# GpSimd's row moves without waits for TensorE, a loading queue with stores between the first row loads, and gathers without a bound

## The chip, the cores and the metric

The kernel runs on one core of a Trainium2 chip. The time is the device time of one execution in microseconds: 1025.71 us is the median of three runs (1023.77, 1025.71 and 1027.04). A core has five engines with instruction queues of their own, TensorE (PE; its weight loads are PEld), VectorE (DVE), ScalarE (ACT), GpSimd (POOL) and SyncE (SP), and 16 DMA engines that all of them share. Queues run in order; they meet only at semaphores.

## The reference

Two transformer layers on 1024 tokens of width 256 (two sequences of 512), each with layer norm, attention and a mixture of experts, all in float32:

```python
x = x + _L0_attn_ref(_layernorm(x), ...)   # 16 heads, a triangular solve over the keys
x = x + _L0_ffn_ref(_layernorm(x), ...)    # 64 experts, top 8, capacity 256 rows each
x = x + _L1_attn_ref(_layernorm(x), ...)   # cumulative sum of phi(k) * v, 16 heads
x = x + _L1_ffn_ref(_layernorm(x), ...)    # 8 experts, top 2
```

The change lies around the first mixture of experts. What it computes:

```python
scores, idx = jax.lax.top_k(probs, TOP_K)                    # 8 experts for each token
xbuf = zeros((E, C, D)).at[e_sorted, pos].set(x[tok_sorted]) # rows sorted by expert
g = einsum('ecd,efd->ecf', xbuf, w_gate); u = einsum('ecd,efd->ecf', xbuf, w_up)
y = einsum('ecf,edf->ecd', silu(g) * u, w_down)
out = zeros((N, D)).at[tok_sorted].add(y_pair)               # each token adds its 8 rows
```

## The kernel before

The program has three blocks, and all five engines meet at a barrier at the end of each: an engine drains its queue, then waits for the others.

**First block: attention of layer 0.** It ends with VectorE choosing the eight experts of the first sequence's tokens (tiles 0 to 3 of 128 tokens) and their slots, while TensorE still works on attention. When those slots are there, GpSimd starts to scatter rows (`scatter`, line 198): one indirect DMA moves the 128 rows of tile `t` for their k-th expert into `expert_rows` in HBM. Experts are sorted within a token, so a row of expert e can only stand among k = 0 to e. There are 8 x 8 = 64 scatters, k by k: 32 for the first sequence, then 32 for the second. The first `EARLY` of them stand in the first block, the others in the second. Between some of them GpSimd waits for a state of TensorE (lines 1193 to 1204, 1527 to 1546); no data depends on these waits.

**Second block: the 64 experts of layer 0.** VectorE computes the slots of the second sequence. TensorE turns the rows of an expert (L1368), multiplies them with the gate and up weights (L1375), turns the hidden rows (L1383) and multiplies with the down weights (L1392); ScalarE applies SiLU, VectorE the product and the copy of the result to `yb` (L1468). The experts run one behind another, software pipelined: `turn` of e + 1, `gate_up` of e, `turn_hidden` of e - 1, `down` of e - 2. SyncE's queue does all loads and stores: weights of two experts at a time into four buffers (L1566, L1567), an expert's 256 rows into one of eight buffers (L1572), and the store of an expert's output (L1576). The load of rows e < 8 waits until all eight scatters of k = e have landed. The order in this queue is written by hand: three weight groups, rows 0 to 5, then a body of eight experts repeated eight times (`steps`; the middle ones as a loop).

At the end GpSimd gathers the outputs back: with row numbers `gather_slots` it fetches 128 rows for one tile and one k into one of 16 buffers `gb` (L1558). The first 16 gathers stand in this block. They wait for the stores that they read (semaphores `s_st`), and, one by one, for a state of TensorE (`s_gu`, `s_y0`). Each has a bound on its row numbers, beyond which it reports an error.

**Third block: layer 1.** VectorE adds the gathered rows into X (L1939), 16 first and then 12 in each of four quarters of two tiles; behind each quarter come its layer norm and linear attention: TensorE turns and projects (L1730, L1742), ScalarE computes features (L1874 to L1880), VectorE a window of cumulative sums (L1950 to L1957), two windows to a quarter, with three gathered adds ahead of the second. GpSimd issues the other 48 gathers (L2116), each as soon as its buffer is free and, at five places of a quarter, only after a state of TensorE. Then layer 1's own scatter (L2132), 23 tiles of expert work (L1815, L1824), each added to `out` by an indirect DMA that accumulates (L2141).

## Time and profile before

| | |
|---|---|
| median of three runs | 1025.71 us (1023.77 to 1027.04) |
| the profiled execution's own time | 1016.34 us |
| its span, first to last instruction | 1014.6 us |
| mean granted TensorE clock | 0.837 |
| busy: PE, PEld, DVE, ACT, POOL | 708.1, 566.9, 549.2, 313.5, 252.2 us |
| DMA | 151.73 MB, mean 150 GB/s |

All durations below are of the one profiled execution. A row of a timeline has the start in us, the duration in us, engine, line, operation, what it writes and reads, a count, and in brackets the idle time of the engine before it with what ended it. "issue" there means that nothing in the profile was waited for. An engine name with a q (SPq, POOLq) is the engine's instruction queue. A DMA's row on POOL is the time in which its descriptors are made, not the transfer.

### The profile page before, as it was taken

What the parts mean: (1) busy time and instruction counts of PE and PEld (TensorE: products, weight loads), DVE (VectorE), ACT (ScalarE), POOL (GpSimd) and SP (SyncE); (2) the same over time, 40 slices, a digit from 0 to 9 for tenths busy, and PEclk for the clock granted to TensorE, in tenths of its full rate; (3) what the DMA queues carried; (4) which work ended last, traced back from release to release, by engine and by line L of the source; (5) the groups of instructions that cost most, each with busy time, mean ns of one, the idle gap of its engine ahead of it and who ended that gap; (6) DMA issues with size and microseconds to landing.
All of it is one profiled execution on the core that took longest, in us unless ns stands there. A gap on an engine that the chain in (4) does not pass through costs nothing. (4 is left out here: it accounts for less than half of the span.)

```text
span 1014.6 us, 17699 instructions
## 1 busy us (share of the span) xinstructions
PE 708.1 (70%) x6542; PEld 566.9 (56%) x6587; DVE 549.2 (54%) x1652; ACT 313.5 (31%) x535; POOL 252.2 (25%) x258
## 2 busy tenths in 40 slices
PE   4858377858757786973156999999205763599995
PEld 2423265446436545842145999999204542599994
DVE  6896986799499679263501333333146675022221
ACT  1004143542444355432022444444003451111110
POOL 6003011120211111016762000000575626023222
PEclk9988779979887898597577999999756675699998
DMA  4981002340631358204947888887422204688760
GB/s 136 137 130 48 0 2 46 156 63 3 199 51 14 125 211 319 96 17 146 320 142 251 288 290 291 294 283 248 130 76 68 81 26 156 244 229 249 221 195 1
DMA packets 75561, 151.73 MB, mean 150 GB/s; under 512 B 12768, under 2 KB 36064, under 8 KB 72544
## 3 DMA queue, kind: packets, MB, share of 16 engines
q1 hardware_dynamic: 62064, 124.27, 39.7%
q0 software_dynamic: 10224, 21.12, 7.4%
q10 hardware_dynamic: 3200, 5.38, 1.6%
q8 instruction: 44, 0.72, 0.3%
q14 instruction: 29, 0.24, 0.1%
HBM read 91.01 MB, written 60.43 MB: 149 GB/s over the span
## 5 line engine op out<-in xcount | busy, mean ns | idle before, releaser
L1375 PE MATMUL scores<-wgu,zero 128*128 128x192 f32 x512 | 98.2, 337 | 3.7 <-DMA wd<-in_wd 3.7
L750 DVE TENSOR_REDUCE block_maxima<-scores 128x10 f32<-128x1280 f32 x64 | 92.3, 1486 | 7.7 <-PE scores L400 6.7
L1032 ACT ACTIVATE E<-scores 128x1280 f32<-128x1280 f32 x64 | 77.3, 1238 | 60.6 <-PE scores L411 32.4
L1476 DVE TENSOR_TENSOR gated_up<-gated,scores 128x192 f32<-128x192 f32 x64 | 22.7, 354 | 123.7 <-ACT gated L1517 123.7
L1375 PEld LDWEIGHTS scores<-wgu,zero 128*128 128x128 f32 x512 | 85.6, 197 | 3.9 <-DMA wd<-in_wd 3.9
L1815 PE MATMUL scores<-xgT,w 128*128 128x128 f32 x736 | 87.8, 278 | 0.0
L1815 PEld LDWEIGHTS scores<-xgT,w 128*128 128x128 f32 x736 | 86.0, 196 | 0.1
L1170 POOL TENSOR_SCALAR_AFFINE_SELECT E<-E 128x256 f32<-128x256 f32 x64 | 27.2, 449 | 205.8 <-ACT E L1032 205.7
L1508 ACT COPY zero<-misc 128x512 f32<-128x512 f32 x64 | 37.5, 586 | 98.3 <-PE misc L1368 98.3
L1392 PE MATMUL scores<-wd,gated_turned 96*128 96x256 f32 x256 | 67.0, 385 | 0.5 <-ACT gated_turned L1504 0.5
L2116 POOL DMA_INDIRECT gb<-expert_outputs,gather_slots x48 | 55.0, 1147 | 33.7 <-DVE X L1939 17.0
L1368 PE MATMUL misc<-cf,xg 128*128 128x128 f32 x256 | 40.3, 281 | 32.7 <-DMA xg<-expert_rows 32.7
L2141 POOL DMA_INDIRECT out<-yb,add_to x23 | 35.5, 1544 | 111.0 <-DVE yb L2079 109.0
L1558 POOL DMA_INDIRECT gb<-expert_outputs,gather_slots x16 | 16.4, 1024 | 171.5 <-DMA expert_outputs<-xnT 164.9
L1468 DVE COPY xnT<-scores 128x512 f32<-128x512 f32 x64 | 44.3, 692 | 25.6 <-PE scores L1392 25.6
L2092 DVE TENSOR_TENSOR cum<-low,scores 128x512 f32<-128x512 f32 x23 | 15.8, 689 | 77.2 <-issue 67.8
L1368 PEld LDWEIGHTS misc<-cf,xg 128*128 128x128 f32 x256 | 32.4, 144 | 41.5 <-issue 19.5
L400 PE MATMUL scores<-cb 128*128 128x128 bf16 x256 | 53.5, 230 | 1.8 <-issue 0.7
L825 DVE TENSOR_TENSOR tmp<-Y,LB 128x120 f32<-128x120 f32 (+35 forms) x244 | 49.7, 242 | 0.3
L834 DVE TENSOR_TENSOR Y<-Y,tmp 128x120 f32<-128x120 f32 (+35 forms) x244 | 49.6, 242 | 0.1
L199 POOL DMA_INDIRECT expert_rows<-stack_q,scatter_slots x32 | 31.5, 984 | 66.4 <-issue 61.3
L1392 PEld LDWEIGHTS scores<-wd,gated_turned 96*128 96x128 f32 x256 | 44.5, 194 | 4.4 <-ACT gated_turned L1504 0.7
(295 smaller groups left out, 1500.4 us busy)
## 6 DMA issues: line engine op xcount, KB each, us to landing
w<-in_w SPq DMA_DIRECT2D x23, 1024.0 KB, 5.0
expert_rows<-zero SPq DMA_DIRECT2D x32, 512.0 KB, 6.2
xg<-expert_rows SPq DMA_DIRECT2D x64, 256.0 KB, 3.2
expert_outputs<-xnT SPq DMA_DIRECT2D x64, 256.0 KB, 3.0
wgu<-in_wgu SPq DMA_DIRECT2D x32, 384.0 KB, 3.6
rows_by_expert<-zero SPq DMA_DIRECT2D x21, 408.0 KB, 6.0
wd<-in_wd SPq DMA_DIRECT2D x32, 192.0 KB, 3.8
w<-in_w ACTq DMA_DIRECT2D x8, 512.0 KB, 10.3
```

The costliest lines, as they stand in the source:

```text
L400: ins = nc.tensor.matmul(scores[:, slot, o + w - P:o + w], identb, mask[c, it], start=False, stop=True)
L750: nc.vector.tensor_reduce(bm[:, c, h, :], scores[:, slot, 0:WIDE].rearrange("p (a n) -> p a n", n=P), AX.X, ALU.max).then_inc(s_fd, 1)
L825: nc.vector.tensor_tensor(part, Yc[:, x, 0:n, k:k + 1].to_broadcast([P, n, w]), LB[:, k:k + 1, k + 1:SB].to_broadcast([P, n, w]), ALU.mult ...
L834: nc.vector.tensor_tensor(below, below, part, ALU.add).then_inc(s_inv, 1)
L1032: nc.scalar.activation(to[:, h, :], scores[:, k % 2, 0:WIDE], ACT.Exp, scale=SCALE).then_inc(s_fa, 1)
L1368: ins = nc.tensor.transpose(misc[:, j % 2, c:c + P], xg[:, j, t, k * P:(k + 1) * P], identf)
L1375: ins = nc.tensor.matmul(scores[:, j % 2, t * 2 * F0:(t + 1) * 2 * F0], xgT[:, j % 2, k, t * P:(t + 1) * P], wgu[:, j // GE, j % GE, k, :] ...
L1392: ins = nc.tensor.matmul(scores[:, j % 2, 1024 + t * D:1024 + (t + 1) * D], hT[:, j % 2, t * P:(t + 1) * P], wd[:, j // GE, j % GE, :], st ...
L1468: nc.vector.tensor_copy(yb[:, j % NY].rearrange("p t d -> p (t d)"), scores[:, j % 2, 1024:1536]).then_inc(s_yv, 1)
L1508: nc.scalar.copy(xgT[:, j % 2].rearrange("p k n -> p (k n)"), misc[:, j % 2, :]).then_inc(s_xt0, 1)
L1815: ins = nc.tensor.matmul(scores[:, j, c:c + P], w13[:, q, k, c:c + P], xgT[:, j, k, :], start=(k == 0), stop=(k == KT - 1))
L2116: pool.indirect_dma_start(out=gb[:, g % NG, :], out_offset=None, in_=ybuf, in_offset=bass.IndirectOffsetOnAxis(ap=ig[:, t, k:k + 1], axis= ...
```

## The change

`EARLY` goes from 16 to 10, so six scatters move behind the first barrier. GpSimd's waits for TensorE's states go in all three blocks; its waits for slots, stores and free buffers stay. Both gathers lose the bound on their row numbers (`bounds_check`, `oob_is_err`). TensorE waits for the slots (`s_idx`) where it waited for the picked weights (`s_w8`) before the first expert. SyncE loads four weight groups before the first rows, puts the stores of experts 0 to 2 between rows 4 to 7, and the first body of eight experts is written out in another order. The whole diff:

```diff
--- before.py
+++ after.py
@@ -40,7 +40,7 @@
 BIG = 32768.0
 LIN_AT = (0, 512, 256)
 LG = 1280
-EARLY = 16
+EARLY = 10
 NQ = 4
 GQ = (N // P // NQ) * 6
 W = N // NQ
@@ -1191,16 +1191,6 @@
                     pool.wait_ge(s_idx, 2)
                     pool.wait_ge(s_zf, 16 * NZ)
                     for g in range(EARLY):
-                        if g == 4:
-                            pool.wait_ge(s_us, 4 * UNITS)
-                        if g == 6:
-                            pool.wait_ge(s_o, 2 * UNITS - 1)
-                        if g == 8:
-                            pool.wait_ge(s_o, 2 * UNITS)
-                        if g == 9:
-                            pool.wait_ge(s_ot, 2 * UNITS)
-                        if g == 11:
-                            pool.wait_ge(s_tr, 10)
                         scatter(pool, g // HT, g % HT, xn0[:, g % HT, :])
 
                 @block.sync
@@ -1357,7 +1347,7 @@
                             ins = nc.tensor.matmul(scores[:, 1, t * E0:(t + 1) * E0], triu if q == t else onesb,
                                                    selb[:, q, :], start=(q == 0), stop=(q == t))
                     ins.then_inc(s_rk, 1)
-                    pe.wait_ge(s_w8, 1)
+                    pe.wait_ge(s_idx, 4)
 
                     def turn(j, i):
 
@@ -1525,24 +1515,10 @@
                 @block.gpsimd
                 def _(pool):
                     for g in range(EARLY, HT * K0):
-                        if g == EARLY + 4:
-                            pool.wait_ge(s_tr, 12)
-                        if g == EARLY + 8:
-                            pool.wait_ge(s_lg, 2)
-                        if g == EARLY + 12:
-                            pool.wait_ge(s_rk, 2)
                         scatter(pool, g // HT, g % HT, xn0[:, g % HT, :])
                     pool.wait_ge(s_idx, 4)
                     for k in range(K0):
                         for t in range(HT):
-                            if t == 0 and k > 5:
-                                pool.wait_ge(s_y0, k - 5)
-                            if t == 1 and k > 1:
-                                pool.wait_ge(s_t, k - 1)
-                            if t == 2 and k > 4:
-                                pool.wait_ge(s_th0, k - 4)
-                            if t == 3 and k > 2:
-                                pool.wait_ge(s_gu, k - 2)
                             scatter(pool, k, HT + t, xn[:, t, :])
                     for j in range(NY):
                         pool.wait_ge(s_st[j], 16 * ((E0 - K0) // NY + (j == 0)))
@@ -1550,15 +1526,11 @@
                         t, k = gather_at(g)
                         if g == NT:
                             pool.wait_ge(s_st[1], 16 * ((E0 - K0) // NY + 1))
-                        if g % 2:
-                            pool.wait_ge(s_gu, min(E0, E0 - 2 + g // 2))
-                        elif g:
-                            pool.wait_ge(s_y0, min(E0, E0 - 5 + g // 2))
                         rows = (E0 - K0 + 1 + k) * CAP
                         pool.indirect_dma_start(
                             out=gb[:, g, :], out_offset=None, in_=ybuf[0:rows],
                             in_offset=bass.IndirectOffsetOnAxis(ap=ig[:, t, k:k + 1], axis=0),
-                            bounds_check=rows - 1, oob_is_err=True).then_inc(s_gb[g], 16)
+                            ).then_inc(s_gb[g], 16)
 
                 @block.sync
                 def _(sp):
@@ -1575,10 +1547,25 @@
                         sp.wait_ge(s_yv, e + 1)
                         sp.dma_start(yb_v[e].rearrange("(p t) d -> p t d", t=2), yb[:, j % NY]).then_inc(s_st[j % NY], 16)
 
-                    for w in range(NW - 1):
+                    for w in range(NW):
                         load_weights(w, w)
-                    for e in range(NB - GE):
+                    for e in range(NB):
+                        if e >= 5:
+                            store(e - 5, e - 5)
                         load_rows(e, e)
+                    store(NB - 5, NB - 5)
+                    for e in range(NB, 2 * NB - GE):
+                        sp.wait_ge(s_t, e - NB + 1)
+                        load_rows(e - NB, e)
+                        if e == NB + 1:
+                            sp.wait_ge(s_y0, GE)
+                            load_weights(0, NW)
+                        if e == NB + 3:
+                            store(4, 4)
+                            sp.wait_ge(s_y0, 2 * GE)
+                            load_weights(1, NW + 1)
+                        if e == NB + 4:
+                            store(5, 5)
 
                     def body(i, first, last):
                         for j in range(NB):
@@ -1595,7 +1582,10 @@
                             if not (first and j < 2):
                                 store((j - 2) % NB, e - 2)
 
-                    steps(sp.Fori, E0 // NB, body)
+                    body(1, False, False)
+                    with sp.Fori(2, E0 // NB - 1) as i:
+                        body(i, False, False)
+                    body(E0 // NB - 1, False, True)
                     store(NB - 2, E0 - 2)
                     store(NB - 1, E0 - 1)
                     for j in range(NY):
@@ -2101,22 +2091,10 @@
                 def _(pool):
                     for g in range(NG, NT * K0):
                         t, k = gather_at(g)
-                        q, r = divmod(g - NG, GQ)
                         pool.wait_ge(s_acc0, g - NG + 1)
-                        if r == 3 and q > 1:
-                            pool.wait_ge(s_oo, QT * (q - 1))
-                        if r == 4 and q:
-                            pool.wait_ge(s_tr, 12 + at_lin(q - 1) + 1)
-                        if r == 7 and q:
-                            pool.wait_ge(s_pr, 2 * q - 1)
-                        if r == 8 and q > 1:
-                            pool.wait_ge(s_tr, 12 + at_ffn(q - 2) + 1)
-                        if r == 10 and q:
-                            pool.wait_ge(s_pr, 2 * q)
                         pool.indirect_dma_start(
                             out=gb[:, g % NG, :], out_offset=None, in_=ybuf,
-                            in_offset=bass.IndirectOffsetOnAxis(ap=ig[:, t, k:k + 1], axis=0),
-                            bounds_check=E0 * CAP - 1, oob_is_err=True).then_inc(s_gb[g % NG], 16)
+                            in_offset=bass.IndirectOffsetOnAxis(ap=ig[:, t, k:k + 1], axis=0)).then_inc(s_gb[g % NG], 16)
                     nc.gpsimd.memset(rows1[:, :, :, D:RW], 0.0).then_inc(s_tok, 1)
                     pool.wait_ge(s_gw, 32)
                     pool.wait_ge(s_tok, 1)
```

GpSimd's queue before, from its first scatter to the end of the first block (L341; `stack_q` holds the first sequence's rows):

```order
L199 DMA expert_rows<-stack_q,scatter_slots 16384x256 [waits slots_zeroed,slots_ready,XR_filled]
L199 DMA expert_rows<-stack_q,scatter_slots 16384x256 x3
L199 DMA expert_rows<-stack_q,scatter_slots 16384x256 [waits solve_u]
L199 DMA expert_rows<-stack_q,scatter_slots 16384x256
L199 DMA expert_rows<-stack_q,scatter_slots 16384x256 [waits attended]
L199 DMA expert_rows<-stack_q,scatter_slots 16384x256
L199 DMA expert_rows<-stack_q,scatter_slots 16384x256 [waits attended]
L199 DMA expert_rows<-stack_q,scatter_slots 16384x256 [waits o_turned]
L199 DMA expert_rows<-stack_q,scatter_slots 16384x256
L199 DMA expert_rows<-stack_q,scatter_slots 16384x256 [waits transposed]
L199 DMA expert_rows<-stack_q,scatter_slots 16384x256 x4
L341 UNCONDITIONAL_BRANCH
```

and after, from the same scatter to the last gathers of the second block:

```order
L199 DMA expert_rows<-stack_q,scatter_slots 16384x256 [waits slots_zeroed,slots_ready,XR_filled]
L199 DMA expert_rows<-stack_q,scatter_slots 16384x256 x9
L341 UNCONDITIONAL_BRANCH
L1515 UNCONDITIONAL_BRANCH [waits barrier_Pool_Activation_PE_DVE_SP_gather]
L199 DMA expert_rows<-stack_q,scatter_slots 16384x256 x22
L199 DMA expert_rows<-xn_moe,scatter_slots 16384x256 [waits slots_ready]
L199 DMA expert_rows<-xn_moe,scatter_slots 16384x256 x31
L1530 DMA gb<-expert_outputs,gather_slots 128x256 [waits y_stored2,y_stored3,y_stored1,y_stored0]
L1530 DMA gb<-expert_outputs,gather_slots 128x256 x7
L1530 DMA gb<-expert_outputs,gather_slots 128x256 [waits y_stored1]
L1530 DMA gb<-expert_outputs,gather_slots 128x256 x7
```

All waits between scatters are gone but that for the second half's slots (`slots_ready`); 10 scatters stand ahead of the block's end and 22 of the first half behind it. The 16 gathers wait for stores only, and in the third block the 48 wait for their buffers alone (`row_added`).

SyncE's queue in the second block before, from the load of row 7 to the store of expert 1 (`rows_moved`k: the scatters of k have landed; `down_copied`: VectorE has copied an expert's output; `rows_turned`: TensorE has turned an expert's rows):

```order
L1572 DMA xg<-expert_rows 128x512 [waits rows_moved7]
L1572 DMA xg<-expert_rows 128x512 [waits rows_turned]
L1566 DMA wgu<-in_wgu 128x768
L1567 DMA wd<-in_wd 96x512
L1576 DMA expert_outputs<-xnT 128x512 [waits down_copied]
L1572 DMA xg<-expert_rows 128x512 [waits rows_turned]
L1576 DMA expert_outputs<-xnT 128x512 [waits down_copied]
```

and after, from the load of row 4 to those of rows 10 and 11:

```order
L1544 DMA xg<-expert_rows 128x512 [waits rows_moved4]
L1548 DMA expert_outputs<-xnT 128x512 [waits down_copied]
L1544 DMA xg<-expert_rows 128x512 [waits rows_moved5]
L1548 DMA expert_outputs<-xnT 128x512 [waits down_copied]
L1544 DMA xg<-expert_rows 128x512 [waits rows_moved6]
L1548 DMA expert_outputs<-xnT 128x512 [waits down_copied]
L1544 DMA xg<-expert_rows 128x512 [waits rows_moved7]
L1548 DMA expert_outputs<-xnT 128x512 [waits down_copied]
L1544 DMA xg<-expert_rows 128x512 [waits rows_turned] x2
L1538 DMA wgu<-in_wgu 128x768 [waits down_done]
L1539 DMA wd<-in_wd 96x512
L1544 DMA xg<-expert_rows 128x512 [waits rows_turned] x2
```

The fourth weight group stood behind the load of row 8 and now stands ahead of row 0. Stores 0, 1, 2 and 3 stood behind it, and now stand ahead of rows 5, 6, 7 and 8.

## Rows read from the trace of the kernel before

**Rows 1.** Two stretches: length, busy us of PE, PEld, DVE, ACT, POOL, clock, DMA.

```profile
510.00:554.00 44.00, 27.05 (x120) 22.85 (x121) 5.25 (x11) 10.04 (x22) 22.37 (x23) 0.78 0.55 181
554.00:712.00 158.00, 158.00 (x1009) 147.32 (x1008) 58.40 (x112) 65.63 (x168) 3.12 (x3) 1.00 0.83 282
```

**Rows 2.** Timeline of GpSimd at the end of the first block.

```profile
470.78 0.97 POOL L199 DMA_INDIRECT expert_rows<-stack_q,scatter_slots  x1 [0.31 <-issue]
474.86 0.97 POOL L199 DMA_INDIRECT expert_rows<-stack_q,scatter_slots  x1 [3.12 <-POOLq L341]
```

**Rows 3.** Line 341, the first block's end: durations in ns, first and last start.

```profile
L341 POOLq DRAIN  x1: 11013/11013/11013, 462.9 to 462.9; - x1
...
L341 DVEq DRAIN  x1: 17/17/17, 465.4 to 465.4; - x1
```

**Rows 4.** Timeline of VectorE and GpSimd around the second half's scatters.

```profile
494.71 0.40 DVE L1452 TENSOR_SCALAR gather_slots<-V8g 128x32 uint32<-128x32 f32 x1
...
512.19 0.97 POOL L199 DMA_INDIRECT expert_rows<-xn_moe,scatter_slots  x1 [4.30 <-issue]
...
540.29 0.97 POOL L199 DMA_INDIRECT expert_rows<-xn_moe,scatter_slots  x1 [0.30 <-issue]
```

**Rows 5.** Timeline of VectorE and TensorE from expert 3's copy to expert 8.

```profile
543.30 0.69 DVE L1468 COPY xnT<-scores 128x512 f32<-128x512 f32 x1 [0.37 <-PE scores L1392]
...
545.44 0.66 PE L1368 MATMUL misc<-cf,xg 128*128 128x128 f32 x4 [2.17 <-DMA xg<-expert_rows]
...
549.75 2.93 PE L1375 MATMUL scores<-wgu,zero 128*128 128x192 f32 x8 [3.66 <-DMA wd<-in_wd]
...
554.11 0.60 PE L1368 MATMUL misc<-cf,xg 128*128 128x128 f32 x4
```

**Rows 6.** The page's DMA issues: count, KB each, median us to landing.

```profile
xg<-expert_rows SPq DMA_DIRECT2D x64, 256.0 KB, 3.2
```

**Rows 7.** Timeline of GpSimd and VectorE, end of the second block.

```profile
706.12 1.07 POOL L1558 DMA_INDIRECT gb<-expert_outputs,gather_slots  x1 [164.85 <-DMA expert_outputs<-xnT]
...
728.12 1.02 POOL L1558 DMA_INDIRECT gb<-expert_outputs,gather_slots  x1 [0.30 <-issue]
...
735.00 6.81 DVE L1939 SCALAR_TENSOR_TENSOR X<-gb,w,X 128x256 f32<-128x256 f32 x17
```

**Rows 8.** Line 1342, the second block's end.

```profile
L1342 POOLq DRAIN  x1: 13496/13496/13496, 720.9 to 720.9; - x1
```

**Rows 9.** Timeline of GpSimd in the third block.

```profile
737.86 4.84 POOL L2116 DMA_INDIRECT gb<-expert_outputs,gather_slots  x1 [0.30 <-DVE X L1939]
743.01 1.02 POOL L2116 DMA_INDIRECT gb<-expert_outputs,gather_slots  x1 [0.30 <-issue]
...
764.18 1.02 POOL L2116 DMA_INDIRECT gb<-expert_outputs,gather_slots  x1 [2.93 <-PE misc L1730]
...
769.99 1.05 POOL L2116 DMA_INDIRECT gb<-expert_outputs,gather_slots  x1 [2.14 <-PE scores L1742]
...
816.64 1.24 POOL L2116 DMA_INDIRECT gb<-expert_outputs,gather_slots  x1 [0.30 <-issue]
```

**Rows 10.** Timeline of ScalarE and VectorE, first and last pair of windows.

```profile
770.58 0.82 ACT L1880 ACTIVATE relu<-scores,bias_lin 128x256 f32<-128x256 f32 x2
...
773.32 0.68 DVE L1950 TENSOR_TENSOR relu<-relu,low 128x512 f32<-128x512 f32 x1
...
775.62 0.87 DVE L1939 SCALAR_TENSOR_TENSOR X<-gb,w,X 128x256 f32<-128x256 f32 x2
...
777.19 0.68 DVE L1950 TENSOR_TENSOR relu<-relu,low 128x512 f32<-128x512 f32 x1
...
813.38 0.82 ACT L1880 ACTIVATE relu<-scores,bias_lin 128x256 f32<-128x256 f32 x2
...
818.60 0.69 DVE L1950 TENSOR_TENSOR relu<-relu,low 128x512 f32<-128x512 f32 x1
```

**Rows 11.** The page's costliest groups: the indirect DMA that adds.

```profile
L2141 POOL DMA_INDIRECT out<-yb,add_to x23 | 35.5, 1544 | 111.0 <-DVE yb L2079 109.0
```

## The prediction

> **What bounds the kernel now.** I read the busy time by stage first, then the timeline of each engine where one stage meets the next. In the stretch from 554 to 712 us TensorE is busy for all of its 158 us at full clock [rows 1]: that is the expert loop in its steady state, 1009 matmuls at 18 an expert are 56 experts, 2.82 us each. Nothing in the change touches it. The stretch ahead of it, 510 to 554, has only 27 of 44 us of TensorE and 22.4 us of GpSimd in 23 scatters [rows 1]: there the experts wait for their rows. So the change can pay at four places: where GpSimd reaches the first block's end, in the row scatters and the first eight experts, in the 16 gathers at the loop's end, and in the quarters of the next layer.
>
> At the first block's end the last scatter before the barrier starts at 470.78, and the next at 474.86 [rows 2]. The drain of GpSimd's queue ends at 462.9 + 11.0 = 473.9, VectorE's at 465.4 [rows 3]: GpSimd alone holds everybody. After the barrier the scatters run back to back, 1.277 us apart (0.97 and 0.30 of issue [rows 4]), with one visible pause: 4.30 us ahead of 512.19 [rows 4], which is the 42nd scatter, the one that in the code waits for the first expert's turned rows. The 64th starts at 540.29 [rows 4]. VectorE had the second half's slots at 495.1 [rows 4], when GpSimd was just done with the first half, so at both places it is GpSimd that is late.
>
> Then SyncE: it waits for the scatters of rows 0 to 7 in order, and everything else stands behind row 7, weight group 3 for experts 6 and 7 too. TensorE, which turns expert 7's rows at 545.44, then waits 3.66 us for that group, and starts expert 6's gate matmuls only at 549.75. They take 2.93 us. Expert 8's rows are turned at 554.11 [rows 5].
>
> **The change, step by step**, against the profiled execution's own 1016.34 us (span 1014.6). The median of the runs shown is 1025.71, 9.4 above it; I take the sum off that median as it stands.
>
> A. Six scatters behind the barrier, no pauses. The tenth scatter starts at 470.78 - 6 x 1.277 = 463.1 and ends at 464.1; GpSimd's drain ended 2.15 us after its last scatter (473.9 - 471.75), so now at 466.2, still after VectorE's 465.4. The next scatter started 0.95 us after the drain, so at 467.2. 54 remain: the 64th starts at 467.2 + 53 x 1.277 = 534.9 instead of 540.29. **5.4 us.** The barrier itself comes 7.7 us earlier, and with it VectorE's slots (487.4), but GpSimd gets to the 33rd scatter only at 467.2 + 22 x 1.277 = 495.3: it stays the bound, and the six moved scatters take back part of what the early barrier gives. Bounds: if the drain costs as at the second block's end (5.3 us, below), A is 2.2; if it shrinks with the count of scatters to nothing, VectorE's 465.4 rules and A is 6.2.
>
> B. The loading queue. With row 7 issued 5.4 earlier, expert 7's rows are turned at 540.0. All four weight groups are in by then (the fourth adds two issues at the start, where SyncE waits for scatters anyway), so expert 6 goes on at once. From the turn of 7 to that of 8 it took 554.11 - 545.44 = 8.67 us; at the loop's pace it is 2.82. **5.8 us.** What could be late next is row 8: it now stands behind the store of expert 3, whose copy ended at 544.0 [rows 5], that is 538.6 after; row 8 is then issued at about 539.1 and, with 3.2 us from issue to landing [rows 6] there at 542.3, against a turn due at 542.9. Just in time. Rows 5 to 7 stand behind stores 0 to 2, whose copies come an expert (5.1 us, four scatters) or so ahead of the scatters they compete with; hidden, but the cover is thin: without it 2.8 us for each expert. If TensorE runs this expert's matmuls as slowly as before (2.93 us, and 8.67 - 3.66 = 5.0 from turn to turn), B falls by up to 2.2. Bounds 3.5 to 6.
>
> The wait of TensorE for the slots in place of the weights costs and gives nothing: it then waits for row 0 until 510.
>
> C. The 16 gathers at the loop's end. The first starts at 706.12 when its stores have landed; the last starts at 728.12, 22.0 after the first. Without the waits for TensorE it is 15 x 1.325 = 19.9 (1.02 and 0.30 [rows 7]). **2.1 us.** This is on the path: the drain of GpSimd ends at 734.4, 5.3 after its last gather's end, the adds of the next block start at 735.0 [rows 7, 8]. The ninth gather waits for the store of expert 57, one expert (2.82 us) after that of 56; eight gathers (10.6 us) cover it.
>
> D. The quarters of the next layer. The first twelve gathers are bound by GpSimd itself. Then it waits 2.93 us at 764.18 and 2.14 at 769.99 for TensorE [rows 9], though 16 buffers let it run ahead. Without these waits it issues all in a row from the third (743.0): the 20th at 743.0 + 17 x 1.325 = 765.5 instead of 769.99, the last at 743.0 + 45 x 1.325 = 802.6 instead of 816.64, and VectorE finds its rows there. What is late next is ScalarE: its features of the first window end at 771.4, where VectorE began at 773.32 [rows 10]: 1.8 gained. The window takes 2.3 (773.32 to 775.62) and three adds in a row 1.2 (0.40 each: 17 in 6.81 [rows 7]), so the second window starts at 775.0 instead of 777.19: 2.2. The next quarters repeat it from that point, TensorE and ScalarE following VectorE, so that each quarter's features come as much earlier as the second window of the quarter before: 2.2, then about 2.9. In the last one they end at 814.2 - 2.9 = 811.3, and the second window starts at 811.3 + 2.3 + 1.2 = 814.8 instead of 818.60 [rows 10]: 3.8. I take **3.6 us**; bounds 0 (contention) and 4.5.
>
> E. Gathers without a bound. No row shows one. The nearest is the gather itself (1.02 us); the cheapest indirect transfer is a scatter at 0.97 [rows 2], the dearest the adding scatter at 1.54 [rows 11]. I take 1.02, no change; 26 gathers are on the path (16 in C, ten in D), so 0.1 us up or down is 2.6 us. Below 0.97 nothing excludes a gain. At 0.7 it would be 8 us.
>
> Sum: 5.4 + 5.8 + 2.1 + 3.6 = 16.9. Profiled 999.4, median **1008.8**; I say 1009.
>
> A gather that starts at 737.86, beside VectorE's 6.8 us of row adds, took 4.84 us instead of 1.02 [rows 7, 9]. The Trainium skill (SBUF — State Buffer, Who interferes with whom) says that a VectorE instruction with two SBUF inputs contends with a GpSimd instruction that reads SBUF, and the one that comes second is blocked. By that rule the trace agrees here, and it speaks against D: gathers that were held back for TensorE now fall beside the adds. If each of the three later quarters met one such collision on the path (3.8 us), D would be gone and the sum 13.3; rival 1 holds that.
>
> **Rivals.**
> 1. Less than forecast: row 8 or the weights land late in the denser start, or collisions like that at 737.86 (3.8 us each) eat D, or the drain costs 5.3 also at the first barrier. For it: the thin cover in B. Against: GpSimd is up to 14 us ahead in D by then. Without D 13.3 are left; with A at 2.2 and B at 3.5, 7.8. Time 1012 to 1018, 0.18.
> 2. More: unbounded gathers at 0.7 us, or a drain that has less to check. 16.9 + 8 = 25: 1001, down to 996. For it: the drain after the 16 gathers is 5.3 us and after the scatters 2.15. 0.14.
> 3. Slower: the gather without a bound is dearer. With p for one, C is 22.0 - 15(p + 0.3), and the last gather of D starts at 743.0 + 45(p + 0.3) against 816.64. At 1.54, the dearest row, the whole comes to 11.2 - 5.6 - 9.2 = -3.6: 1029. From 1.48 on nothing is gained; at 1.6 it is 11.2 - 6.5 - 11.9 = -7.2: 1033. Nothing speaks for it but that no row shows it. 0.04.
> 4. The waits removed were met anyway and the time stays: against it stand the pauses that the rows show. 0.02.
>
> **How the numbers follow.** The forecast (gain 12 to 21, 1005 to 1014 by itself) 0.62. The range from 1001.5 to 1018.5 holds it, most of rival 1 and half of rival 2. 0.3% (about what a measurement of this kernel can tell from no change) is 3.1 us: faster 0.94, same 0.02, slower 0.04.
>
> **What would show it.** GpSimd's 64th scatter near 535; no wait for expert weights at gate matmuls 6, and expert 8 turned near 543; the gathers at the loop's end 1.33 apart, and the next block's first add near 722; no pause in the 48 gathers, ScalarE in place of the transfers ahead of VectorE's windows, the last window 16 to 17 us earlier. I am wrong if TensorE waits for rows 5 to 9, if gathers are not 1.02 us, or if the drains take other times.

## The result: 3.1% slower, and the profile after

| | before | changed |
|---|---|---|
| median of 4 runs each | 1024.91 us (1023.77 to 1027.04) | 1056.28 us (1054.98 to 1060.68) |
| profiled execution, its span | 1016.34 us, 1014.6 | 1060.68 us, 1059.0 |
| TensorE's mean granted clock in it | 0.837 | 0.824 |

The ratio is 1.031 (1.027 to 1.035). I had forecast 1009, so the sign is wrong and the time lies 38 us outside my range. By stage (us from, length, busy time and count of TensorE, its weight loads, VectorE, ScalarE and GpSimd, then clock, DMA share, GB/s), the changed kernel beside [rows 1]:

```profile
510.00:554.00 44.00, 11.62 (x42) 9.32 (x42) 11.30 (x82) 3.37 (x5) 28.14 (x29) 0.54 0.43 150
554.00:712.00 158.00, 147.49 (x918) 135.56 (x919) 53.68 (x103) 60.81 (x156) 2.91 (x3) 0.96 0.79 268
```

Where TensorE had 27 us of work in the 44, it now has 11.6. GpSimd's timeline shows that it is not the pitch of the scatters (start, length, instruction, idle time before it and what ended it):

```profile
480.98 0.97 POOL L199 DMA_INDIRECT expert_rows<-stack_q,scatter_slots  x1 [14.23 <-POOLq L341]
...
517.16 0.97 POOL L199 DMA_INDIRECT expert_rows<-xn_moe,scatter_slots  x1 [8.43 <-DVE gather_slots L1442]
...
556.69 0.97 POOL L199 DMA_INDIRECT expert_rows<-xn_moe,scatter_slots  x1 [0.30 <-issue]
```

The pauses for TensorE are gone as intended, the pitch is still 1.27 us [rows 4], and yet the 64th scatter starts at 556.69 instead of 540.29 [rows 4]: GpSimd waits 14.2 us at the barrier ([rows 2]: 3.1 before), and then 8.4 us for slots that it had found ready in [rows 4]. Both waits end late because other engines are late. The other engines' timeline at the first block's end, around the ranks and in the expert loop:

```profile
468.60 0.26 DVE L893 RECIPROCAL rec<-scores 128x16 f32<-128x16 f32 x1 [11.49 <-remote]
...
496.80 1.57 PE L1347 MATMUL scores<-selb,cb 128*128 128x64 bf16 x26 [6.12 <-issue]
...
512.33 0.42 DVE L1431 TENSOR_SCALAR slot<-scores 128x256 f32<-128x256 f32 x1 [15.58 <-remote]
...
538.03 1.92 PE L1365 MATMUL scores<-wgu,zero 128*128 128x192 f32 x8
...
544.07 2.90 PE L1365 MATMUL scores<-wgu,zero 128*128 128x192 f32 x8 [1.55 <-issue]
...
560.84 0.33 ACT L1507 ACTIVATE gated<-scores 128x192 f32<-128x192 f32 x1 [16.91 <-remote]
561.20 0.35 DVE L1466 TENSOR_TENSOR gated_up<-gated,scores 128x192 f32<-128x192 f32 x1 [24.85 <-ACT gated L1507]
561.61 0.66 PE L1373 MATMUL scores<-cf,gated_up 128*96 128x128 f32 x2 [14.64 <-DVE gated_up L1466]
```

VectorE's L893, which takes up TensorE's products before the barrier, waited 3.03 us in the trace of before. TensorE ends the ranks at 498.4, and VectorE, which needs nothing else, reads them at 512.3. The gate matmuls of expert 1 end at 539.95, and the activation that reads them, ScalarE's second, starts at 560.8, 20.9 us later; TensorE has by then done those of expert 2 as well (544.07 to 546.97), which ScalarE takes up at 563.0. "Remote" is how the view names a releaser that it cannot find. In both cases GpSimd was in an unbroken run of scatters that ended shortly before: 22 of them, up to 508.7, and 32, up to 557.7. The third block has it twice more, beside gathers that run from 763.0 to 816.1 with hardly a pause:

```profile
789.61 8.04 PE L1732 MATMUL scores<-xnT,w_lin 128*128 128x256 f32 x24 [0.68 <-issue]
...
805.61 0.84 ACT L1864 ACTIVATE low<-scores,minus_bias 128x256 f32<-128x256 f32 x2 [14.54 <-remote]
...
821.07 0.84 ACT L1864 ACTIVATE low<-scores,minus_bias 128x256 f32<-128x256 f32 x2 [13.23 <-remote]
```

The 24 matmuls are both windows' projections and end at 797.7. ScalarE reads the first window's at 805.6, in the middle of the run of gathers, and the second window's, for which it is free from 807.8 on, only at 821.1. So two results that were both there were not handed over together.

These four waits (ranks, gate, two windows) are 60 us of idle time on engines that wait for TensorE. A fifth lies at the end of the second block, beside its 16 gathers (731.8 to 751.7):

```profile
751.04 0.33 ACT L1507 ACTIVATE gated<-scores 128x192 f32<-128x192 f32 x1 [10.20 <-remote]
```

In the profile of before VectorE and ScalarE have no wait over 1 us that ends "remote" in these stages. But an unbroken run does not hold everything: in the run of 32 scatters ScalarE took up its first three results of TensorE within 0.7 us, the fourth (expert 2's turned rows, done at 538.2) in mid-run and 5.1 us late, and only the fifth was held to the end:

```profile
543.34 0.58 ACT L1498 COPY zero<-misc 128x512 f32<-128x512 f32 x1 [7.38 <-PE misc L1358]
```

### The profile page after: what moved, and what is told of

It reads as the page before. It is cut to its first block and busy times, and to the rows that moved or that the text cites. A ratio compares the mean times of both kernels' runs of the same rounds, so it can differ in the third digit from the quotient of the medians.

```text
span 1059.0 us, 17621 instructions
## 1 busy us (share of the span) xinstructions
PE 711.8 (67%) x6542; PEld 565.8 (53%) x6587; DVE 547.8 (52%) x1652; ACT 313.0 (30%) x535; POOL 246.1 (23%) x258
## 5 line engine op out<-in xcount | busy, mean ns | idle before, releaser
L2095 POOL DMA_INDIRECT gb<-expert_outputs,gather_slots x48 | 50.3, 1048 | 38.3 <-DVE X L1929 26.1
L1530 POOL DMA_INDIRECT gb<-expert_outputs,gather_slots x16 | 15.3, 955 | 178.7 <-DMA expert_outputs<-xnT 174.1
```

What stands on the lines that cost most here:

```text
L2095: pool.indirect_dma_start(out=gb[:, g % NG, :], out_offset=None, in_=ybuf, in_offset=bass.IndirectOffsetOnAxis(ap=ig[:, t, k:k + 1], axis= ...
```

## Experiments

**Theory.** While GpSimd issues indirect DMAs one behind the other, results of TensorE can be held: the work is done, but the engines that wait for it are told late, most often only when GpSimd has stopped. I call this the hold-up. The waits for TensorE that the change removed were, unknown to me, the stops. **Rivals:** the new loading queue or the unbounded gathers cost the time; any wait, even one already met, would do; only a wait on TensorE's own semaphore would do. Medians and ratios are against the kernel before on the chip of the same call.

### First call: put back, take out, replace

**e1**, the change with all of the removed waits and EARLY 16 put back:

```diff
-EARLY = 10
+EARLY = 16
+                        if g == 4:
+                            pool.wait_ge(s_us, 4 * UNITS)
...
+                            if t == 1 and k > 1:
+                                pool.wait_ge(s_t, k - 1)
...
+                        if r == 7 and q:
+                            pool.wait_ge(s_pr, 2 * q - 1)
```

> The changed kernel with all of GpSimd's waits for TensorE put back (EARLY 16 again); the loading queue with stores between the first row loads and the unbounded gathers stay. Theory (long unbroken runs of GpSimd's indirect DMAs hold back what TensorE reports to the other engines, and the waits had cut these runs): the gaps of 14 to 17 us behind L1347 and L1365 and in the third block go, and what is left of my forecast is B and C, 5.8 + 2.1 us: 1017 us (1010 to 1023). Rival (the loading queue or the gathers without a bound are what costs the time, the waits were harmless): the time stays near 1056 us, and DVE still idles over 10 us behind the ranks of TensorE.

**e2**, the kernel before with only the waits gone (as the change in that, old queue and `bounds_check` kept):

> The kernel before with only GpSimd's waits for TensorE taken out (and EARLY 10, TensorE's wait on the slots as in the change); old loading queue, bounded gathers. Theory: as slow as the whole change or slower, 1055 to 1065 us, with the same gaps (about 15 us in front of DVE's reading of the ranks, about 15 us in the expert stage, 2 x 13 us in the third block). Rival (loading queue or unbounded gathers cost the time): A and D of my forecast alone, 1024.9 - 9 = about 1016 us.

**e3**, the change with a wait that is already met at each of those places:

```diff
+                            if t == 1 and k > 1:
+                                pool.wait_ge(s_idx, 2)
```

> The whole change, but where the kernel before had a wait for TensorE GpSimd has a wait that was met long before (slots of the first half ready). It tells a wait's instruction from a wait's pause. If GpSimd must really stop for TensorE to get through: 1056 us as the change, with the same gaps. If any wait between two DMAs is enough to let TensorE through: near 1010 us, GpSimd's DMAs still at their pitch of 1.27 us and no gap over 5 us on DVE or ScalarE in front of TensorE's results.

**e4**, the change with GpSimd waiting for its own transfer after every eighth:

```diff
+                        if g and g % 8 == 0:
+                            pool.wait_ge(s_gb[g // HT - 1], 16 * HT)
...
+                            if t == 0 and k and k % 2 == 0:
+                                pool.wait_ge(s_gb[k - 1], 16 * NT)
```

> The whole change, but GpSimd stops after every 8th indirect DMA until its own last one has landed: a pause that has nothing to do with TensorE (in all about 15 pauses of some 2 to 3 us). If what counts is that the run of DMAs is broken: TensorE's results come through at each pause, gaps of at most about 8 us in place of 15, and a time of 1015 to 1040 us. If what counts is that GpSimd waits for TensorE's own work (its results are taken in step): 1056 us or more, since the pauses only add to GpSimd's chain.

| | us | ratio (95%) |
|---|---|---|
| before | 1025.0 | |
| e1 waits back | 1017.9 | 0.993 (0.991 to 0.995) |
| e2 only waits gone | 1047.3 | 1.022 (1.019 to 1.025) |
| e3 waits already met | 1058.0 | 1.031 (1.027 to 1.035) |
| e4 own landing | 1027.6 | 1.003 (1.002 to 1.005) |

e1 and e2 point at the waits: with them the change takes 7 us less than before, without them alone the kernel loses 22. In both the waits go together with `EARLY` (16 with them, 10 without); e4, which keeps `EARLY` at 10, shows that `EARLY` is not the cause of most of it. e3 is as slow as the change, so a wait instruction that does not stop GpSimd does nothing; its ranks reach VectorE as late as in the change:

```profile
510.77 0.42 DVE L1441 TENSOR_SCALAR slot<-scores 128x256 f32<-128x256 f32 x1 [16.89 <-remote]
```

e4 wins back 29 of the 31 us with stops that have nothing to do with TensorE. Its ranks wait

```profile
493.25 0.42 DVE L1433 TENSOR_SCALAR slot<-scores 128x256 f32<-128x256 f32 x1 [3.65 <-remote]
```

and four of its six stops among the scatters are as short as this one (the other two are 4.59 and 5.43 us):

```profile
525.51 0.97 POOL L199 DMA_INDIRECT expert_rows<-xn_moe,scatter_slots  x1 [2.23 <-DMA expert_rows<-xn_moe,scatter_slots]
```

In e4 VectorE's L893 still waits 8.57 us, so these stops cure most of the hold-up and not all. e2 was 8 us better than I had expected at least, which left room for a part of the queue or of the gathers (below).

### Second call: before once more, the queue alone, and each place

**e5** is the kernel before, unchanged. **e6** is before with the new loading queue only. **e7** is the change with the waits of the third block put back (the `r == 3` to `r == 10` lines), **e8** with all but these.

> The kernel before once more, for a second profile: the profiled execution of the first was 1016.3 us beside a median of 1024.9. If the same hold-up of TensorE's results is in the kernel before too, and was only absent from the profiled execution: a profiled time near 1024 us, with over 7 us of idle time in front of DVE's L893 (3.03 in the first profile). If the difference is elsewhere: L893 waits about 3 us again.

> The kernel before with the new loading queue alone (stores between the first row loads, the fourth weight group at the start); all waits and bounds of before. By my forecast's B: 5.8 us less, 1019 us. By the traces of the kernel with the waits back (first to last turn of the experts 197.9 us against 199.8): 2 us less, 1023 us. Rival (the new queue costs time by itself): 1026 us or more.

> The whole change with the waits for TensorE put back in the third block's gathers only. Theory (each block's unbroken run costs for itself): the two gaps of 14.5 and 13.2 us of ScalarE there go, from the end of the block before to the first scatter of rows it takes 104 to 106 us in place of 129, and the whole is 1056 - 19 to 25 = 1031 to 1037 us. Rival (one hold-up early on puts everything out of step, or the third block's waits are of no use since it waits for VectorE's adds anyway): near 1056.

> The whole change with the waits put back in the first two blocks only (EARLY 16), none in the third. Theory: the gaps behind the ranks and in the expert stage go, those of the third block stay: 1018 + 19 to 25 = 1037 to 1043 us. Rival: near 1018 us if the third block's gaps only follow from the earlier ones.

| | us | ratio (95%) |
|---|---|---|
| before | 1024.6 | |
| e5 before again (one run) | 1025.6 | |
| e6 queue alone | 1021.9 | 0.997 (0.996 to 0.999) |
| e7 waits in the third block | 1041.3 | 1.014 (1.011 to 1.018) |
| e8 waits in the first two | 1034.9 | 1.009 (1.006 to 1.013) |

From e1's 1017.9, leaving out the third block's waits costs 17 us and the first two blocks' 23, together 40, about the 38 between e1 and the change: the runs of each block cost their share by themselves (e1 and the change were timed on other chips than e7 and e8, and e7 also has `EARLY` 10). Both times miss my brackets, 1031 to 1037 and 1037 to 1043, though on the theory's side of the rival's. e8 still has both gaps of the third block (13.86 and 13.94 us ahead of ScalarE's features) and none over 9 us ahead of it. The new queue alone gives 2.7 us.

e5 was the surprise. The kernel before has the hold-up too, on a smaller scale, and the profile that I had forecast from did not show it. Its timeline:

```profile
464.29 0.26 DVE L893 RECIPROCAL rec<-scores 128x16 f32<-128x16 f32 x1 [8.79 <-remote]
...
496.62 0.42 DVE L1441 TENSOR_SCALAR slot<-scores 128x256 f32<-128x256 f32 x1 [3.76 <-remote]
...
528.74 0.33 ACT L1517 ACTIVATE gated<-scores 128x192 f32<-128x192 f32 x1 [1.81 <-PE scores L1375]
...
530.27 0.66 PE L1368 MATMUL misc<-cf,xg 128*128 128x128 f32 x4 [1.35 <-issue]
530.76 1.47 PE L1375 MATMUL scores<-wgu,zero 128*128 128x192 f32 x8
...
532.06 0.38 PE L1383 MATMUL scores<-cf,gated_up 128*96 128x128 f32 x2
532.28 1.03 PE L1392 MATMUL scores<-wd,gated_turned 96*128 96x256 f32 x4
...
534.33 0.97 POOL L199 DMA_INDIRECT expert_rows<-xn_moe,scatter_slots  x1 [0.30 <-issue]
535.10 1.05 PE L1368 MATMUL misc<-cf,xg 128*128 128x128 f32 x4 [1.79 <-DMA xg<-expert_rows]
535.95 2.77 PE L1375 MATMUL scores<-wgu,zero 128*128 128x192 f32 x8
...
537.27 0.33 ACT L1517 ACTIVATE gated<-scores 128x192 f32<-128x192 f32 x1 [4.40 <-remote]
537.50 0.36 ACT L1504 COPY gated_turned<-scores 96x256 f32<-96x256 f32 x1
537.64 0.35 DVE L1476 TENSOR_TENSOR gated_up<-gated,scores 128x192 f32<-128x192 f32 x1 [8.19 <-ACT gated L1517]
537.75 0.59 ACT L1508 COPY zero<-misc 128x512 f32<-128x512 f32 x1
537.91 0.68 DVE L1468 COPY xnT<-scores 128x512 f32<-128x512 f32 x1
538.04 0.97 POOL L199 DMA_INDIRECT expert_rows<-xn_moe,scatter_slots  x1 [2.73 <-remote]
```

This is the clearest picture of it. TensorE does the gate matmuls (done at 532.2), turns the hidden rows, does the down projection (done at 533.3) and goes on to the next expert's rows at 535.1. It isn't stopped. ScalarE's activation and its two copies and VectorE's product and copy need four different results of it (done from 532.2 to 536.2) and all start between 537.27 and 537.91, in a bunch. One held result is enough for that: the activation waits for the gate matmuls, ScalarE's copies stand behind it in its queue, VectorE's product needs the activation, and VectorE's copy stands behind the product. GpSimd had issued its last scatter at 534.33 (to 535.3) and stood at a wait for the same gate matmuls (`s_gu`); two microseconds into that stop ScalarE and GpSimd were both told. So what is held is the news of a finished result, not the engine.

### Third call: other stops, and a different chip

**e9** moves the waits to where TensorE's results are due; **e10** waits in the first two blocks for the engines that use the result (in the third only two of a quarter's five waits are changed so); **e11** replaces e4's waits by work, five fills of 2.87 us together (each waits for the one before it); **e12** is the change on the old queue.

```diff
 e9
-                        if g == 6:
+                        if g == 2:
                             pool.wait_ge(s_o, 2 * UNITS - 1)
...
-                            if t == 1 and k > 1:
-                                pool.wait_ge(s_t, k - 1)
+                            if t == 2 and k > 1:
+                                pool.wait_ge(s_t, k)
 e10
-                                pool.wait_ge(s_gu, k - 2)
+                                pool.wait_ge(s_h, k - 2)
 e11
+                        if g and g % 8 == 0:
+                            pause(pool)
...
+        def pause(pool):
+            for _ in range(5):
+                if n_pz[0]:
+                    pool.wait_ge(s_pz, n_pz[0])
+                n_pz[0] += 1
+                nc.gpsimd.memset(pz[:], 0.0).then_inc(s_pz, 1)
```

> The kernel with the waits back, new loading queue and unbounded gathers (1017.9 us), but with the waits moved to where TensorE's results come due: GpSimd stops for the two products, the turned output and the turned rows at its scatters 2, 3, 4 and 7 (before at 4, 6, 8, 9 and 11), for the ranks at EARLY + 10, for the turned rows of expert k - 1 in expert k, and once in the scatters of the third block. Theory (results are held while a run of indirect DMAs lasts, so a stop right where a result is due lets it through): the idle time in front of L893 falls from 8.5 to about 3 us, that behind the ranks from 3.5 to under 1, the gap of 4.8 us in the third block to about 2, and the time falls by 5 to 10 us: 1008 to 1013. Rival (the stops cost GpSimd as much as they give): 1018 to 1022.

> As the kernel with the waits back (1017.9 us), but in the first two blocks GpSimd waits for the engine that uses TensorE's result (VectorE's or ScalarE's semaphore) and not for TensorE's; the third block's waits stay, one of them on ScalarE's copy. If what counts is that GpSimd stops in step with the work: 1015 to 1022 us. If it must be TensorE's own semaphore that GpSimd waits for: near 1040 us, with the gaps of about 15 us of the change in the first two blocks.

> The whole change, but after every 8th indirect DMA GpSimd fills a scratch tile five times (about 2.5 us of its own work, no wait for anyone). It is the run with its own landings awaited (1027.6 us), with work in place of the wait. If it is the issuing of indirect DMAs that holds TensorE's results back: they come through in each pause and the time is 1022 to 1035 us. If GpSimd must stand still at a wait: 1056 us or more.

> The whole change with the old loading queue: waits gone, gathers unbounded. The whole change was 1056.3 us and the kernel with only the waits gone 1047.3, although the new queue alone gives 2.7 us. If the new queue is worse once the waits are gone (row loads behind stores that come late): about 1044 us (1047.3 less what the unbounded gathers give). If the unbounded gathers, with their closer pitch (1.26 against 1.38 us), make the third block's hold-up longer: about 1055 us.

| | us | ratio (95%) |
|---|---|---|
| before | 1015.9 | |
| e9 tight waits | 1028.0 | 1.013 (1.010 to 1.016) |
| e10 consumers' waits | 1011.8 | 0.996 (0.994 to 0.998) |
| e11 work as pause | 1019.5 | 1.004 (1.002 to 1.006) |
| e12 no waits, old queue | 994.8 | 0.980 (0.977 to 0.982) |

Neither side of e12 had expected 994.8. (The 1.38 us in its text is too much: bounded gathers stand 1.325 us apart [rows 7].) The first column of times explains it: on this chip the kernel before takes 1015.9 us, not 1024 to 1025, and 1015.9 is near what my profile of before had shown (1016.34). In none of the four traces do VectorE or ScalarE have a "remote" wait over 1 us in these stages. In e12 GpSimd issues 54 scatters from 469.1 to 537.8 without one stop, and in the middle of them the ranks take

```profile
483.24 1.57 PE L1347 MATMUL scores<-selb,cb 128*128 128x64 bf16 x26 [4.42 <-DVE selb L1426]
...
484.92 0.42 DVE L1431 TENSOR_SCALAR slot<-scores 128x256 f32<-128x256 f32 x1 [1.74 <-PE scores L1347]
```

0.1 us from TensorE to VectorE, against 14.0 in the change's profile. So e9, e10 and e11 ran where there was nothing to cure, and tell only what stops cost: e9's six stops in the expert rows held GpSimd for 22 us (this view: what GpSimd waited for from 497 to 562 us, total, times, longest),

```profile
POOL expert_rows L199 <- PE misc L1366: 22.2, 6, 4.7
```

and the kernel lost 12 us; its expectation failed, and for the hold-up it says nothing.

### Fourth and fifth call: the same kernels on two more chips

**f1** is the change, unchanged. **f2** and **g2** are e12, **f3** and **g1** are e10, **g3** is e1.

> The change as it is, on the chip that this call gets. Theory (the hold-up depends on the chip): where the kernel before takes about 1024.5 us, 1056 us with the gaps; where it takes about 1016 us, none of the gaps and my forecast's gain, 1016 - 17 = about 999 us. Rival (the change is slow everywhere): 1047 to 1056 us on either.

> The kernel without waits and bounds on the old loading queue, 994.8 us on the third chip. Theory: 995 us again if the kernel before takes 1016 us; if the kernel before takes 1024.5 us, 1044 to 1055 us with gaps of about 15 us. Rival (this pairing of queue and gathers is free of the hold-up by itself): 995 to 1003 us also beside a kernel before of 1024.5.

> Waits in the first two blocks for the engines that use TensorE's results (1011.8 us on the third chip). On a chip with the hold-up: 1016 to 1022 us if a stop in step with the work is enough, near 1040 us if the wait must be on TensorE's own semaphore. On a chip without it: 1012 us again, which tells nothing of this.

> Beside a kernel before of 1024 to 1025 us (a chip with the hold-up): 1016 to 1022 us if a stop in step with VectorE and ScalarE is enough, near 1040 us if GpSimd must wait on TensorE's own semaphore. Beside a kernel before of 1015 to 1017 us: 1010 to 1012 us as in the two runs there.

> Beside a kernel before of 1024 to 1025 us: 1044 us if the new queue is what makes the change 9 us slower than the kernel with only the waits gone (1047.3), 1053 to 1056 us if it is the closer pitch of the unbounded gathers. Beside a kernel before of 1015 to 1017 us: 995 us again.

> Beside a kernel before of 1024 to 1025 us: 1017 to 1018 us again. Beside a kernel before of 1015 to 1017 us: the waits cost there what they hold GpSimd back, 1009 to 1012 us by the kernel with waits for the other engines, so 15 to 18 us more than the change (994).

| | with the hold-up: us, ratio | without it: us, ratio |
|---|---|---|
| before | 1024.4 to 1025.0 in four calls | 1015.9 and 1017.2 |
| the change | 1056.3, 1.031 (1.027 to 1.035) | 994.2, 0.979 (0.976 to 0.983) |
| no waits, old queue | 1053.4, 1.029 (1.026 to 1.031) | 995.1, 0.979 (0.976 to 0.982) |
| consumers' waits | 1024.3, 1.000 (0.998 to 1.001) | 1009.6, 0.993 (0.991 to 0.996) |
| TensorE's waits back | 1016.3, 0.992 (0.990 to 0.994) | not run |

The change is 3.1% slower on one chip and 2.1% faster on another, both beside the kernel before on the same chip. g1 answers e10's question: stops in step with VectorE and ScalarE are worth most of it (1024.3, far from 1040), though 8 us less than the waits for TensorE; it missed my bracket by 2 us. g3 repeats e1, 1.6 us faster. g2 against e2 says which other part hurts once the waits are gone: unbounded gathers take the kernel from 1047.3 to 1053.4 (on different chips, each beside a before of 1024.4 to 1025.0). That their closer pitch is the reason is my reading and not shown. The 3 us more of the change (1056.3), which would be the new queue's, are within the intervals. With the waits in place the same two parts are gains: 2.7 for the queue (e6), 4 for the gathers (e6 to e1, 1021.9 and 1017.9, on two chips).

The traces sort as the times do. In all twelve profiles taken where before takes 1024.4 to 1025.0, VectorE's L893 waits 8.5 to 11.6 us and ends "remote", e1 and g3 with all stops included. In the seven where it takes 1015.9 or 1017.2, and in my first profile of before, no "remote" wait of VectorE, ScalarE or GpSimd between the first scatter and layer 1's experts is over 1 us.

No version beats before on both kinds of chip by as much as e1 does on one and the change on the other; e1 is the safe choice of those run where the hold-up is.

## Why the prediction was wrong

The profile that I predicted from is of an execution without the hold-up; the times that I took the sum off, and the result, are of executions with it. f1, the change on a chip without it, is therefore where my steps can be read one by one. Its own time was 988.47 us, span 986.7, the lowest of its four runs (median 994.2).

**A (5.4 us): right.** I had put 71.8 us from the tenth scatter to the 64th (463.1 to 534.9); f1 has 71.6, and before it was 77.2 (463.1 to 540.29 [rows 4]): 5.6. The pauses that went were two: beside the 4.30 us that I had called the one visible pause, the trace of before has 1.34 us ahead of 481.02; my sum held both. The next scatter starts 2.87 us after the tenth's end, and no pause follows:

```profile
461.23 0.97 POOL L199 DMA_INDIRECT expert_rows<-stack_q,scatter_slots  x1 [0.30 <-issue]
465.08 0.97 POOL L199 DMA_INDIRECT expert_rows<-stack_q,scatter_slots  x1 [2.87 <-POOLq L341]
...
532.81 0.97 POOL L199 DMA_INDIRECT expert_rows<-xn_moe,scatter_slots  x1 [0.30 <-issue]
```

**B (5.8 us): 4.1 in the trace, about 1 in the time.** TensorE no longer waits for the weights of expert 6, and expert 8 is turned at 543.04:

```profile
538.48 0.66 PE L1358 MATMUL misc<-cf,xg 128*128 128x128 f32 x4 [2.76 <-DMA xg<-expert_rows]
538.98 2.60 PE L1365 MATMUL scores<-wgu,zero 128*128 128x192 f32 x8
...
543.04 0.60 PE L1358 MATMUL misc<-cf,xg 128*128 128x128 f32 x4
```

From turn to turn 4.56 us instead of 8.67 [rows 5]. The gate matmuls still run slowly after their wait (2.60 us), the bound that I had named. But f2, the same kernel with the old queue in the same call, has the wait that B removes,

```profile
543.92 2.93 PE L1365 MATMUL scores<-wgu,zero 128*128 128x192 f32 x8 [3.99 <-DMA wd<-in_wd]
```

with 9.50 us from turn to turn, and its median is only 1.0 us above f1's (995.1 and 994.2, within the intervals); with the waits kept the queue was worth 2.7 (e6). So B happened where I had put it, and as a price it was too high. What takes the rest back is not shown.

**C (2.1 us) and E (none): 3.1.** The 16 gathers start within 18.9 us, 1.26 apart. A gather without a bound takes 0.95 us where one with a bound took 1.02 [rows 7]; E is a small gain that I had put at zero.

```profile
693.95 0.99 POOL L1530 DMA_INDIRECT gb<-expert_outputs,gather_slots  x1 [160.17 <-DMA expert_outputs<-xnT]
...
712.86 0.95 POOL L1530 DMA_INDIRECT gb<-expert_outputs,gather_slots  x1 [0.30 <-issue]
```

**D (3.6 us): about 12, the term that was mis-sized.** From the 16th gather to the first scatter of the next layer's rows it takes 100.0 us (712.9 to 812.9) where it took 112.2 (728.1 [rows 7] to 840.3). That scatter, before and in f1:

```profile
840.30 1.08 POOL L2132 DMA_INDIRECT rows_by_expert<-rows_ffn,slots  x1 [20.95 <-DVE slots L1988]
```

```profile
812.91 1.06 POOL L2110 DMA_INDIRECT rows_by_expert<-rows_ffn,slots  x1 [24.74 <-DVE slots L1978]
```

I had counted the two waits of GpSimd for TensorE, 5.1 us, and let ScalarE give back part of them. But GpSimd's longer waits in the quarters were for VectorE's adds, and most of these went too. What GpSimd waited for there, before and then in f1:

```profile
POOL gb L2116 <- DVE X L1939: 17.0, 8, 7.1
...
POOL gb L2116 <- PE misc L1730: 2.9, 1, 2.9
POOL gb L2116 <- PE scores L1742: 2.1, 1, 2.1
```

```profile
POOL gb L2095 <- DVE X L1929: 10.1, 11, 7.1
```

7.1 of both is the start of the block, so 9.9 us became 3.0. With the 5.1 that is the 12, but it is a sum and not a proof: 48 cheaper gathers lie in the same stretch, and no run separates them from the waits. f2 and e12 took 101.2 and 100.1 us there, so the size is no accident of f1's profile. The collision with the adds that rival 1 feared came once (4.45 us at 723.74), as before, and not again.

So without the hold-up each of the four steps happened and the sum was too small: the medians of f1's call differ by 23.1 us, I had 16.9. A and C held, D was too small by 8 us, and B was too large. The steps as read in the trace come to 24.9; that trace is of f1's fastest execution, 27.9 us below the profiled one of before.

**What failed** is a step that I took without writing it down as one. I costed each removed wait by how much sooner GpSimd gets on ("Without these waits it issues all in a row"), and took for granted that TensorE's results reach VectorE and ScalarE as promptly as before, whatever GpSimd does meanwhile. Where the hold-up exists this is false: e1 and e2 show 38 and 22 us of it, and e4 that stops of GpSimd that have nothing to do with TensorE win back 29. My rival on the slow side was the price of an unbounded gather; that price went the other way. My one trace even spoke for the step: from 512 us on GpSimd issued 23 scatters in a row for 29 us, and TensorE's results were taken up meanwhile. That this held for executions of one kind only, the trace could not show.

There was a sign. "The median of the runs shown is 1025.71, 9.4 above it; I take the sum off that median as it stands." Nine microseconds between a profiled execution and all timed ones is three times the spread of the timed ones. e5 shows what they were: L893 waits 8.79 us instead of 3.03, the ranks 3.76 instead of 1.73, ScalarE's activation 4.40, and the ranks of the third block 4.97. A second profile would have shown that the program has two behaviours and that I was looking at the faster one.

**Open.** What differs between the chips is not shown: the code and the data are the same, and TensorE's mean clock up to 440 us is 0.85 in the first profile of before and 0.86 in e5. Each chip served in one call only, so that it is the chip, and not something else that differed from call to call, is an inference as well; within a call nothing changed sides. Nor is the path shown on which the results are held, or whether it is GpSimd's issuing or the traffic of its DMAs that holds them; stopping GpSimd stops both. The release does not only come at a stop of GpSimd: those at 543.34, 751.04 and 805.61 came inside a run, those of L893, the ranks, the gate and the second window 2 to 5 us after a run's last DMA. No length from which on a run holds results could be read: in e5 they were passed on at 528.7 and held from 532.2 on in the same run. Whether work instead of a wait is stop enough was not answered, since e11 ran where there was no hold-up. TensorE's waits put back were not run on a chip without it.

## What to carry to other kernels

Ask of a wait not only what it delays but what it interrupts: one that looks useless can be the only stop in a long run of DMA issues, and others may live on that stop. Before taking such waits out, take one out and look in the trace for engines that idle behind TensorE's finished work with a releaser that the view cannot name ("remote"). And when a profiled execution is faster or slower than every timed one by more than their spread, profile again, on another chip if there is one, before working out any sum: here the same edit was +3.1% on one chip and -2.1% on another.

## What the runs showed of the hardware

- Results of TensorE reached the waiting engines late while GpSimd issued indirect DMAs every 1.26 or 1.27 us: ranks done at 498.4 were read at 512.3, a gate result done at 539.95 at 560.8, and a projection done by 797.7 at 821.1, by an engine free from 807.8 on. On other chips the ranks were read 0.1 us after in a longer run (54 scatters). The late delivery was in all twelve profiles of three chips and of the result, and in none of the seven of two others, nor in the profile ahead of the prediction.
- TensorE goes on meanwhile if its next instructions need nobody: in e5 it turned the next rows at 535.1, while its gate result, done at 532.2, was taken up at 537.3.
- A wait of GpSimd that is already met does not help (e3, 1058.0 us); stops until its own last DMA has landed do (e4, 1027.6).
- GpSimd spends 0.95 us on an indirect gather without a bound, and 1.02 on one with a bound.
- A stop of GpSimd for its own last scatter cost 2.23 to 2.25 us in four of e4's six, and 4.59 and 5.43 in the other two.
